# Layer 0's second half adds its rows into a table that holds x, and layer 1 takes the LayerNorm of gathered rows

## The reference

```python
h = relu(layernorm(x)); x = x + L0(h)   # twice: h = relu(segment_sum((h @ W.T + b)[src], dst))
h = relu(layernorm(x)); x = x + L1(h)   # g = (1+eps)*h + segment_sum(h[dst], src)
                                        # g = relu(g @ W1.T + b1) @ W2.T + b2; layernorm(g)*gamma + beta
h = relu(layernorm(x)); x = x + L2(h)   # layernorm(h + relu(h @ Ws.T + bs + mean_neigh(h @ Wn.T + bn)))*gamma + beta
h = relu(layernorm(x)); x = x + L3(h)   # segment_sum(relu(concat(h[src], h[dst]) @ W.T + b), src)
```

## Time and profile before

| | |
|---|---|
| timed runs, median of 3 | 2800.5 us |
| profiled execution, span | 2943.3 us, the only time known of it |
| PE, VectorE, ACT, POOL busy | 86%, 68%, 48%, 59% of the span |
| granted clock, mean over the span | 0.967 |
| DMA | 388.08 MB, mean 132 GB/s |
| layer 0, first half | about 393 to 709 us |
| layer 0, second half | about 726 to 1166 us |
| layer 1 | about 1188 to 1766 us |
| layers 2 and 3 | about 1783 to 2355, 2390 to 2943 us |

### The profile page before, as it was taken

The page is one execution under the profiler, slowest core; times in us unless marked ns, Lnnn a source line. Parts: engine busy times, 40 slices in busy tenths (PEclk is TensorE's granted clock), DMA queues, the critical chain, the costliest instruction groups (busy, mean ns, idle before and its releaser), DMA issues. The chain is left out here.

```text
span 2943.3 us, 48010 instructions
## 1 busy us (share of the span) xinstructions
PE 2538.7 (86%) x13886; PEld 2157.9 (73%) x13886; DVE 2010.9 (68%) x5233; ACT 1401.3 (48%) x2905; POOL 1737.8 (59%) x1867
## 2 busy tenths in 40 slices
PE   4555269997878776799999987999999979999998
PEld 3444158886767665799999986888888768888886
DVE  7777656663545444487878886888888846666666
ACT  1555235543656554555555533433333245555554
POOL 1666335554565555577777756877777555555554
PEclk9999999998999898899999998999999989999999
DMA  8777533334333443434334324433333245555553
GB/s 251 203 206 208 159 106 112 111 119 121 104 113 119 129 129 106 126 116 131 109 114 121 112 73 129 129 117 113 115 116 109 80 135 156 151 152 153 151 154 116
DMA packets 146046, 388.08 MB, mean 132 GB/s; under 512 B 34372, under 2 KB 34692, under 8 KB 145315
## 3 DMA queue, kind: packets, MB, share of 16 engines
q0 software_dynamic: 101408, 304.38, 35.0%
q1 hardware_dynamic: 43442, 80.04, 8.9%
q10 hardware_dynamic: 1056, 2.10, 0.2%
HBM read 261.83 MB, written 149.12 MB: 140 GB/s over the span
## 5 line engine op out<-in xcount | busy, mean ns | idle before, releaser
L824 PE MATMUL b_po<-parts,b_Thi 128*128 128x512 f32 x320 | 144.7, 452 | 72.0 <-issue 40.9
L1565 PE MATMUL c_pu<-c_Zhi,parts 128*128 128x256 f32 x640 | 182.9, 286 | 5.3 <-DVE c_Zlo L1490 5.3
L1567 PE MATMUL c_pu<-c_Zhi,parts 128*128 128x256 f32 x640 | 182.4, 285 | 0.0
L1566 PE MATMUL c_pu<-c_Zlo,parts 128*128 128x256 f32 x640 | 181.3, 283 | 0.0
L845 POOL DMA_INDIRECT f_Gsrc<-rows,indexS x80 | 79.2, 990 | 167.3 <-PE f_phsrc L2061 161.3
L1979 ACT ACTIVATE f_Mhi<-f_pm 128x512 fp32r<-128x512 f32 x80 | 47.9, 599 | 266.4 <-DVE f_pm L2012 259.8
L2003 DVE TENSOR_TENSOR f_Hlosrc<-f_phsrc,f_Hhisrc 128x512 fp32r<-128x512 f32 x80 | 55.4, 692 | 168.0 <-ACT f_Hhisrc L1973 137.3
L814 DVE SCALAR_TENSOR_TENSOR b_carry<-b_carry,keylastD,b_pt 128x4 f32<-128x4 f32 x80 | 17.4, 218 | 212.6 <-PE b_pt L1282 127.8
L1727 ACT CAST d_Hhi<-d_ph 128x512 fp32r<-128x512 f32 x80 | 46.8, 585 | 227.3 <-PE d_ph L1841 222.3
L849 POOL DMA_INDIRECT h<-a_rows,indexD x80 | 80.5, 1006 | 124.0 <-ACT a_rows L1148 116.5
L1457 ACT ACTIVATE c_pu<-c_pu,c_b1col 128x256 f32<-128x256 f32 x160 | 61.8, 450 | 164.6 <-PE c_pu L1567 164.6
(11 more groups left out here) (461 smaller groups left out, 9817.4 us busy)
## 6 DMA issues: line engine op xcount, KB each, us to landing
rows<-r_xt SPq DMA_DIRECT2D x40, 520.0 KB
h<-q_zerorow SPq DMA_DIRECT2D x80, 256.0 KB
r_xt<-in_x SPq DMA_DIRECT2D x80, 256.0 KB
selrowsD<-selD SPq DMA_DIRECT2D x1, 2640.0 KB
selrowsS<-selS SPq DMA_DIRECT2D x1, 2640.0 KB
q_keyrowD<-in_dst POOLq DMA_DIRECT2D x1, 2560.0 KB, 17.8
q_keyrowS<-in_src POOLq DMA_DIRECT2D x1, 2560.0 KB
o_wstage<-in_L_W ACTq DMA_DIRECT2D x2, 1024.0 KB
```

The lines of the kernel that those rows point to most:

```text
L824: ins = pe.matmul(out, hi[:, c, :], whi[:, c, :], start=start and c == 0, stop=False, skip_group_check=preset)
L1565: pe.matmul(psum_u[:, o, :], g.Whi[2][:, c, cols], Zhi[:, c, :], start=c == 0, stop=False)
L1566: pe.matmul(psum_u[:, o, :], g.Whi[2][:, c, cols], Zlo[:, c, :], start=False, stop=False)
L1567: ins = pe.matmul(psum_u[:, o, :], g.Wlo[2][:, c, cols], Zhi[:, c, :], start=False, stop=c == C - 1)
```

## The change

Layer 0's first half also copies x, tile by tile, into a new plain table `g.x1` (rows of 512), on SP's queue. The second half no longer gathers x and takes no statistics; it stores relu(output) with an indirect DMA that adds to `g.x1`, right after each tile. Rows that are not the last of their node are added to spare rows behind the table instead of being skipped. Its selection matrix is made on VectorE with one operation, as in the first half. Layer 1 gathers from `g.x1`, whose rows carry no scale and bias: VectorE takes the statistics of G and X after they have landed, POOL makes four scales and biases for a pair in one operation each (`scales_in`, placed between `lengths_y` and `keep_x`), and ACT's LayerNorm waits for them. In layer 1 the bias b2 is no longer added by VectorE but preset into the output by an ACT copy.

```diff
+    g.x1 = nc.dram_tensor("plain1", [N + 1 + SPARE, D], F32, kind="Internal").ap()
...
+                sp.dma_start(g.x1[N:N + 1, :], zero_row[0:1, 0:D]).then_inc(q_end, 16)
+                for n in range(ADD_RING):
+                    sp.dma_start(g.x1[N + 1 + n * P:N + 1 + (n + 1) * P, :], zero_row[:, 0:D]).then_inc(q_end, 16)
...
+                        turns = [P, NT // ADD_RING, ADD_RING]
+                        step(dve.tensor_scalar(spare[:, :].rearrange("p (a r) -> p a r", r=ADD_RING),
+                                               g.node_f[:, 0:ADD_RING].unsqueeze(1).broadcast_to(turns),
+                                               float(N + 1), None, ALU.add))
+                        step(dve.tensor_tensor(tmp_c[:, :], scol[k][:, 0, :], spare[:, :], ALU.subtract))
+                        step(dve.tensor_tensor(tmp_c[:, :], tmp_c[:, :], ownerc[k][:, :], ALU.mult))
+                        step(dve.tensor_tensor(g.index[k][:, :, 1], tmp_c[:, :], spare[:, :], ALU.add))
...
+def add_rows(pool, table, at_rows, rows):
+    return pool.indirect_dma_start(table, bass.IndirectOffsetOnAxis(ap=at_rows, axis=0), rows, None,
+                                   compute_op=ALU.add)
...
+                for t in range(NT):
+                    sp.wait_ge(s_rows, t + 1)
+                    sp.dma_start(g.x1[t * P:(t + 1) * P, :], io.x[t * P:(t + 1) * P, :]).then_inc(s_copy, 16)
+                sp.wait_ge(s_copy, 16 * NT)
...
-            def residual(T):
-                s = T.slot(U)
-                wait(pool, s_rows, T.t - 3)
-                fetch(pool, xr[s][:, :], io.x, index(g, "D", T, 1)).then_inc(s_x[s], 16)
-
-            def scales(T):
-                some = slice(T.slot(RING), T.slot(RING) + QUAD)
-                ln.make_scales(pool, T, neg_half, rows[:, some, SCALE])
-                ln.make_biases(pool, T, rows[:, some, SCALE], rows[:, some, BIAS])
-
             def store(T):
                 s = T.slot(RING)
+                pool.wait_ge(s_rows, T.t + 1)
                 if second:
-                    pool.wait_ge(ln.s_bias, T.t // QUAD + 1)
+                    add_rows(pool, g.x1, index(g, "D", T, 1), rows[:, s, :]).then_inc(s_put[s], 16)
...
             def body(i):
-                if second:
-                    for u in range(RING):
-                        if u % QUAD == 0:
-                            at(i, u, -QUAD, RING, NT, scales)
-                        at(i, u, 4, RING, NT, start_fetch)
-                        at(i, u, 2, RING, NT, residual)
-                        at(i, u, -QUAD, RING, NT, store)
-                else:
-                    for u in range(U):
-                        at(i, u, -2, U, NT, store)
-                        at(i, u, 4, U, NT, start_fetch)
+                for u in range(U):
+                    at(i, u, -2, U, NT, store)
+                    at(i, u, 4, U, NT, start_fetch)
...
-            def add_x(T):
-                s, x, r = T.slot(2), T.slot(U), T.slot(RING)
+            def relu_rows(T):
+                s, r = T.slot(2), T.slot(RING)
                 dve.wait_ge(s_prod, T.t + 1)
-                dve.wait_ge(s_x[x], 16 * (T.use(U) + 1))
 
                 wait(dve, s_put[r], 16 * T.use(RING))
-                dve.scalar_tensor_tensor(rows[:, r, 0:D], psum_o[s][:, :], 0.0, xr[x][:, :],
-                                         ALU.max, ALU.add).then_inc(s_rows, 1)
-
-            def norm_rows(T):
-                dve.wait_ge(s_rows, T.t + 1)
-                ln.statistics(dve, T, rows[:, T.slot(RING), 0:D])
-
-            def finish_rows(T):
-                ln.finish(dve, tick, T)
+                dve.tensor_scalar(rows[:, r, :], psum_o[s][:, :], 0.0, None, ALU.max).then_inc(s_rows, 1)
...
-                        at(i, u, 3, RING, NT, select)
+                    at(i, u, 3, RING, NT, select)
...
-                        at(i, u, -1, RING, NT, norm_rows)
-                    if second:
-                        at(i, u, -1, RING, NT, finish_rows)
...
-        src, out = g.xs[0], g.xs[1]
+        src, out = g.x1, g.xs[1]
...
+            def scales_in(T):
+                J = item(T, 0)
+                some = slice(J.slot(8), J.slot(8) + 4)
+
+                wait(pool, s_Gn, T.t - 2)
+                wait(pool, s_own, T.t - 2)
+                ln_in.make_scales(pool, J, neg_half, scale_in[:, some])
+                ln_in.make_biases(pool, J, scale_in[:, some], bias_in[:, some])
...
+                    at(i, pair, 6, U, NT, scales_in)
...
+                s, g_at, x_at = T.slot(U), item(T, 0).slot(8), item(T, 1).slot(8)
+                act.wait_ge(ln_in.s_bias, T.use(2) + 1)
+                nc.scalar.activation(G[s][:, :], G[s][:, :], ACT.Relu, bias=bias_in[:, g_at:g_at + 1],
+                                     scale=scale_in[:, g_at:g_at + 1]).then_inc(s_Gn, 1)
                 wait(act, s_summed, T.t - 1)
-                nc.scalar.activation(H[T.slot(2)][:, :], X[s][:, 0:D], ACT.Relu, bias=X[s][:, BIAS:BIAS + 1],
-                                     scale=X[s][:, SCALE:SCALE + 1]).then_inc(s_own, 1)
+                nc.scalar.activation(H[T.slot(2)][:, :], X[s][:, :], ACT.Relu, bias=bias_in[:, x_at:x_at + 1],
+                                     scale=scale_in[:, x_at:x_at + 1]).then_inc(s_own, 1)
+
+            def preset(T):
+
+                wait(act, s_rows, T.t - 3)
+                nc.scalar.copy(psum_o[T.slot(4)][:, :], b2[:, :]).then_inc(s_preset, 1)
...
+                        at(i, u, 2, U, NT, preset)
...
-                o = psum_o[T.slot(4)][:, :]
                 dve.wait_ge(s_prod, T.t + 1)
-                dve.tensor_tensor(o, o, b2[:, :], ALU.add).then_inc(s_biased, 1)
-                dve.wait_ge(s_biased, T.t + 1)
-                ln_y.statistics(dve, T, o)
+                ln_y.statistics(dve, T, psum_o[T.slot(4)][:, :])
+
+            def norm_in(T):
+                s = T.slot(U)
+                for n, landed, tile in ((0, s_G, G), (1, s_X, X)):
+                    J = item(T, n)
+                    dve.wait_ge(landed[s], 16 * (T.use(U) + 1))
+                    wait(dve, ln_in.s_mean, J.t - 1)
+                    dve.sem_inc(tick, 1)
+                    ln_in.statistics(dve, J, tile[s][:, :])
+
+            def finish_in(T):
+                for n in range(2):
+                    ln_in.finish(dve, tick, item(T, n))
...
-                    for stage in (norm_y, center, new_rows, norm_rows, finish_rows):
+                    for stage in (norm_y, center):
+                        for u in (pair, pair + 1):
+                            at(i, u, -2, U, NT, stage)
+                    for u in (pair, pair + 1):
+                        at(i, u, 6, U, NT, norm_in)
+                        at(i, u, 6, U, NT, finish_in)
+                    for stage in (new_rows, norm_rows, finish_rows):
```

More of the change, by code:

```diff
@@ L980, in layer0 @@
     GR = NT // U
-    QUAD, RING = 8, 16 if second else 4
+    RING = ADD_RING
     with ExitStack() as ctx:
@@ L993, in layer0 @@
         Thi, Tlo = e.ring("Thi", 2, [P, C, P], F32R), e.ring("Tlo", 2, [P, C, P], F32R)
-        rows = e.sb("rows", [P, RING, EXT if second else D], F32)
-        xr = e.ring("xr", U, [P, D], F32) if second else None
-        ln = Norm(e, "ln", True, QUAD) if second else None
+        rows = e.sb("rows", [P, RING, D], F32)
         W = None if second else Weights(nc, e, g, [(2, io.L1_W1), (3, io.L1_W2)])
@@ L1015, in layer0 @@
         s_Gn = e.sem("s_Gn")
-        s_G, s_x, s_put = e.sems("s_G", U), e.sems("s_x", U), e.sems("s_put", RING)
+        s_G, s_put = e.sems("s_G", U), e.sems("s_put", RING)
+        s_copy = None if second else e.sem("s_copy")
         s_sel = e.sem("s_sel")
@@ L1052, in store @@
             def store(T):
                 s = T.slot(RING)
+                pool.wait_ge(s_rows, T.t + 1)
                 if second:
-                    pool.wait_ge(ln.s_bias, T.t // QUAD + 1)
+                    add_rows(pool, g.x1, index(g, "D", T, 1), rows[:, s, :]).then_inc(s_put[s], 16)
                 else:
-                    pool.wait_ge(s_rows, T.t + 1)
-                put_rows(pool, g.xs[0] if second else g.h1, index(g, "D", T, 2), rows[:, s, :], N - 1)\
-                    .then_inc(s_put[s], 16)
+                    put_rows(pool, g.h1, index(g, "D", T, 2), rows[:, s, :], N - 1).then_inc(s_put[s], 16)
@@ L1074, in _ @@
             if second:
-                pool.memset(one_f[:, :], 1.0)
-            pool.memset(neg_half[:, :], -0.5).then_inc(s_const, 1)
+                pool.memset(one_f[:, :], 1.0).then_inc(s_const, 1)
             for s in range(2):
                 pool.memset(carry[s][:, :], 0.0).then_inc(s_const, 1)
-            if second:
-                pool.memset(rows[:, :, BIAS + 1:EXT], 0.0).then_inc(s_const, 1)
-            pool.wait_ge(s_const, 4 if second else 3)
+            pool.wait_ge(s_const, 3 if second else 2)
@@ L1110, in hot_row @@
                     .then_inc(e_hot, 1)
-            def sel_row(T):
```

(21 more changed lines are left out.)

41 lines of the change are left out of this document (20 added, 21 removed).

## The result

Against 2800.3 us before, the changed kernel takes 2918.7 us (median of 4 runs, 2915.5 to 2920.2): ratio 1.0425, 95% interval 1.0413 to 1.0438. The forecast was slower, 2883 us, with a range to 2915; the time lies 36 us above the one and 4 above the other. The profiled execution, forecast at 2920, spans 2913.7 us. It is itself the fastest of the four timed ones, so the sign that the forecast named, a distance of 143 us between span and timed runs, can't show in this pair. The distance of 142.8 us before has another likely cause: there is a chip on which the kernel before takes 2941 us in its timed runs. The profile before fits an execution there in span (2943.3 us) and granted clock (0.967; the timed runs there have 0.967 to 0.970, those on three other chips 0.977 to 0.980), and its timed runs do not.

What follows compares the result with a forecast made beforehand. PE was taken to bound all but layer 0's second half, which had 106 us of profile-only stalls. From the median, 2800.5 - 13 (pace) - 12 (stage end) + 106 (layer 1) + 2 (copies, preparation) gave 2883 us; range 2775 to 2915.

Steps and rivals of the forecast that it cites:

- the sign that the forecast named: Whole kernel, after: if timed runs keep a 143 us distance to the profiled span, the stalls were real.
- the 106 us: Layer 0's second half, before: stalls taken as in the profiled execution and mostly not in timed runs.
- layer 1's loss: Layer 1: from the fifth on, 35 pairs pay 3.03 us each, 106 us.
- the ring: Layer 1: POOL's scales, additions, stores, gathers, landing and VectorE's statistics wait in a circle, 17.0 us a pair against 13.97.
- The stage starts some 4 us later, which the free pairs take back: Layer 1's start: first rows need statistics, some 4 us; first pairs run free at about 13 us; net nothing.
- The copies and the preparation: Layer 0's first half and preparation: copies of x hidden, 0 to 2 us at the end; preparation 1; together 2.
- rival 4: Layer 0's first half: copies delay its gathers by 0.2 us a tile, 16 us more; no chance given.
- The end of the second half: Layer 0's second half, last carry to next stage: 23.5 us falls to the first half's 11.2, 12 less.
- rival 1: Layer 0's second half: stalls are the kernel's own, in timed runs too; 2777 us, faster; chance 0.16.
- rival 2: Layer 1: the ring doesn't bind, pace stays at 13.97 us a pair; 2781 us, faster; chance 0.09.
- Rival 3: Layer 0's second half: accumulating transfer slow, 5 us each, adds 91 us; 2971 us; chance 0.06.
- The DMA page's landing: Layer 1's gathers: 2.6 us by the page's fit, making the ring 16.0 us and the loss 71 instead of 106.

Runs made afterwards that it cites:

- l1_only: Kernel before with only layer 1 as changed, layer 0 as before, gathering from the old table: 2933.7 us, ratio 1.047.
- before_look: The kernel before, unchanged, run again for its profile on a chip that also times it: 2797.4 us, span 2795.6 us.
- copy_at_once: Changed kernel with x copied to the new table by one transfer instead of 80 paced copies: 2970.2 us, ratio 1.061.
- plain_store: Changed kernel with overwriting stores instead of accumulating ones, x left out of layer 0's result: 2917.7 us, ratio 1.0424.
- quad4: Kernel before with batches of four tiles instead of eight in layer 0's second half: 2797.1 us, ratio 0.9993.
- a third order: Changed kernel with VectorE's gathered statistics behind the new rows' statistics: 20.8 us a pair, 3087.7 us, ratio 1.050 where the kernel before takes 2941.

## Why the forecast was wrong

Right were its direction, the mechanism in layer 1 and the choice to leave the 106 us out of the timed sum. The step that failed is the size of layer 1's loss: the forecast had 106 us, and `l1_only` measured 133. Of the 27 us between them 16 are in the ring and 11 in the start of the stage, which the sum had put at nothing. The other 9 of the 36 us are in layer 0 (6 + 2, and 1 for the second half's pace).

1. **"Sum 17.0 us against 13.97": the term that was furthest off.** The ring is 17.45 us. The landing is 3.86 instead of 3.6, above both single ones of the earlier trace rows but inside the ends that the forecast gave it. The additions are 2.65 instead of 2.50, and statistics to power 1.40 instead of 1.3. 35 pairs by 0.45 us are 16 of the missing 36 us.
2. **"The stage starts some 4 us later, which the free pairs take back": the term put at nothing.** From the stage's first memset to its first `first` are 29.6 us (1013.59 to 1043.15), against 1175.65 to 1194.61 = 19.0 in the profile before and 19.7 in `before_look`. The first pairs take 13.4, 15.3 and 14.7 us, as against 13.6, 15.6 and 14.0 before: nothing is given back. The forecast had the ring of four tiles gathered before the first wait. But the first `scales_in` already stands ahead of the second pair's gathers on POOL, and before they went out behind the first pair's at once. These are the first pair's last gather and the second pair's first one, after and then in `before_look`:

```profile
1018.32 0.95 POOL L863 DMA_INDIRECT c_X<-plain,indexS  x1 [0.30 <-issue]
1027.86 1.08 POOL L914 TENSOR_TENSOR c_scalein<-c_lninvar,c_neghalf 128x4 f32<-128x4 f32 x1 [8.59 <-DVE c_lninvar L904]
...
1029.39 1.02 POOL L863 DMA_INDIRECT c_G<-plain,indexS  x1 [0.16 <-issue]
```

```profile
1032.02 0.95 POOL L845 DMA_INDIRECT c_X<-rows,indexS  x1 [0.30 <-issue]
1033.28 0.96 POOL L845 DMA_INDIRECT c_G<-rows,indexS  x1 [0.31 <-issue]
```

   This is 11 us (10 by `before_look`).
3. **The copies and the preparation, 2 us.** The first half takes 308.9 us from carry to carry instead of 304.2, the preparation 3 more. Five waits of ACT for a gather (13.2 us in all in the changed kernel, none in `before_look`) say that the copies make some land late, and `copy_at_once` shows the same collision enlarged; no run has the changed layer 0 without the copies. This was rival 4, true at a third of its size. Together it is 6 us over the forecast.
4. **The end of the second half, 12 us.** From the last carry to layer 1's first memset are 13.6 us instead of 23.5: a gain of 10 us and not 12. An accumulating store takes POOL 0.6 us longer and lands 2 us later; in `plain_store` the stretch is 11.6 us. This is 2 us.
5. **The stalls.** I read 106 us as the recorder's, since nothing else seemed able to hold 142.8 us. Their sum and place were read rightly, and leaving them out gave the right base, but with luck: the likely cause, a profile from another chip than the timed runs, was not among those that I had weighed. Three profiles with the old layer 0 (`l1_only`, `quad4`, `before_look`) have no such stalls, which speaks against the reading that I took from the NOTIFIC — the notification-queue block page of the Trainium skill (section "7.1 Overflow: three behaviours, one of which stalls the engine"), that the records' path can push back on the engine. Whether recording has a part in the stalls on the one chip is not shown. Where before takes 2941, rival 1's premise, stalls in the timed runs too, is true by the estimate above.
6. **Rivals 2 and 3.** The ring binds, so rival 2 falls. Rival 3 needed an accumulating transfer of more than five times a plain one; it is 2.6 times, by the estimate below, and its 2.1 us a tile stay under the 3.2 that the forecast allowed. (The rival's price was added up unevenly: 80 x 1.1 is 88 and not 91, and its 2971 is 2883 + 88.)
7. **The DMA page's landing** (The DMA: Bandwidth & Descriptors page of the Trainium skill, "Anatomy of one DMA — SWDGE (gpsimd) path"), an estimate of 2.6 us, would have made the ring 16.0. The trace has 3.86 from the last issue's start to the statistics, so the measurement decides against it here; the plain scattered stores of `plain_store`, with 2.8 us to landing, come near it.

The range, 2862 to 2912 for this case, was built from the landing's and the power's ends alone. Its upper end was added up too low: a landing of 4.0 and a power of 1.7 instead of 1.05 add 0.4 + 0.65, so the ring would be 18.05 us and not 17.8, the loss 143, and the end 2920 instead of 2912. That would have held the 2918.7, but by luck: the ring, at 17.45, is well inside its ends. The range had no width for the start of a stage or for layer 0, and those 19 us (11 + 6 + 2) are what carried the time past 2915.

## What to carry to other kernels

When a step begins to wait for data that used to be only passed on, draw every in-order queue that the waiting instruction stands in, each added wait once on each engine: here POOL's gave 17.45 us, VectorE's 16.9, and a third order 20.8, while by the sums of busy time PE's 14 would have stood. Removing the longest ring gains only the distance to the next. Work that is moved to where its engine stands idle anyway can be had for nearly nothing, as in the last two orders here (the stores in the wait for a variance, the selections in the wait for ACT's high part). And when a profile's span is 5% over the timed median, ask first whether it is of another chip's execution, before any cause is found in it.

## What the hardware showed unexpectedly

- An accumulating indirect transfer of 128 rows by 2 KB occupies POOL for 1575 ns instead of 1005, lands after 4.8 us instead of 2.8, and costs the DMA engines 2.6 times as much, by the estimate below. These are POOL's rows by line, 700 to 1010 us, of the changed kernel and of `plain_store`, and then the queue's row of each for that stretch (packets, MB, share):

```profile
L867 POOL DMA_INDIRECT plain<-b_rows,indexD x80 | 126.0, 1575 | 91.7 <-DVE b_rows L1187 91.7
...
q0 software_dynamic: 17324, 40.18, 74.2%
```

```profile
L872 POOL DMA_INDIRECT plain<-b_rows,indexD x80 | 80.4, 1005 | 136.9 <-DVE b_rows L1187 134.2 <-DMA plain<-b_rows,indexD 2.5 <-issue 0.3
...
q0 software_dynamic: 12240, 40.12, 40.6%
```

  The bytes are the same. (0.742 - 0.406) x 310 / 80 = 1.3 us more of all sixteen engines go to each accumulating transfer, on top of 0.406 x 310 / 154 = 0.8 for a plain one. This takes the gathers beside them to cost the same in both.
- The same kernel takes 2798 to 2800 us on three chips and 2941 on another (2937 to 2943 in 12 of its 13 runs there). Two forms of the same layer seem to differ in whether they feel it: the new second half runs there at 3.89 to 3.92 us a tile without a stall, and the old one stalls for 104 to 106 us in the one profile that fits that chip.
